# A decoder layer with 64 experts: the token table made by one-hot matmuls on chip for every batch, softplus passes moved between slots, routing steps reordered

## The chip, the cores and the metric

The kernel runs on one core of a Trainium2 chip. The metric is device time in microseconds (us) of one execution; lower is better. A core has TensorE (PE, matrix products), VectorE (DVE), ScalarE (ACT), GpSimd (POOL) and SyncE (SP), which run their own instruction queues in order and meet at semaphores.

## The reference, cut to what matters

```python
x = _layernorm(x + attn(x))                       # lightning attention, 16 heads, chunks of 128
x = _layernorm(x + mamba(ctx_1024, x))            # selective scan, below
x = _layernorm(x + ffn(x))                        # 64 experts, below
...
# mamba: B=4, L=512, inner 512, state 16
dt = jax.nn.softplus(dt + dt_proj_b[None, :, None])
def step(state, inp):
    d, b, c, u = inp
    dA = jnp.exp(d[..., None] * A)
    state = state * dA + (d * u)[..., None] * b[:, None, :]
    y = jnp.einsum('bdn,bn->bd', state, c)
...
# ffn: 2048 tokens, top 8 of 64 experts, 256 places an expert
topw, topi = jax.lax.top_k(probs, K)
flat_e = topi.reshape(-1)
oh = jax.nn.one_hot(flat_e, E, dtype=jnp.int32)
pos = jnp.take_along_axis(jnp.cumsum(oh, axis=0), flat_e[:, None], axis=1)[:, 0] - 1
xe = jnp.zeros((E, C, H), x.dtype).at[flat_e, pos].set(x_rep, mode='drop')
```

Each choice of a token gets the next place at its expert; a choice behind the 256th is dropped. The kernel needs the inverse: for each of the 64 x 256 slots, the token that sits in it (or a spare row, where the slot is empty).

## The kernel before

It has two blocks. `mixers` computes attention, scan and routing for 4 batches of 512 tokens; `experts` then gathers the token rows of one expert after another, multiplies, and adds the results to the token rows by indirect DMAs.

In `mixers` the selective scan sets the frame. A batch has 4 tiles (of the 512 inner channels), a tile 8 slots, so there are 128 slots. In each slot GpSimd makes one product (`inputs`, two partition groups at once, 128x1024), ScalarE makes two exponentials (`decays`), VectorE runs two scans and one product (`scan`), and TensorE sums over the state (`sum_states`). Every other piece of work is written by hand between these, engine by engine, in the loops `for b, for c (tile), for k (slot)`. The products are at most three slots apart from the sums (`WORK`), the decays two from the scan.

Other work in the slots: the attention of 128 tokens per tile (projections, rotation on GpSimd in slot 5, scores, values, first norm); in tile 2 the convolution for the next batch; in tile 3 the softplus of half of the next batch's channels (`EARLY`), in tile 0 that of the other half (`LATE`); in tiles 0 and 1 the second norm and the routing of the batch before.

The softplus is `soften` (ScalarE), `exponentials` (ScalarE), `logs` (ScalarE: one logarithm and two Identity passes a channel tile), `soft_parts` (GpSimd), `excess` (ScalarE), `soft_rest` (GpSimd), `steps` (ScalarE), `steps_of_u` (GpSimd); then SyncE copies the result to other partitions (`copy_steps`), which the next products and decays wait for (`spread`).

PSUM for everything but the scan is a ring of three banks: `to_fill` takes the next bank and waits until its last content was drained, in the order in which TensorE fills them.

The routing (VectorE): `shift_logits`, `choose` (top 8), `count_places` on TensorE, `find_slots` (slot number of each choice), `tell_slots`. For batches 0 to 2 the tokens are then written to a table in memory by indirect DMAs from GpSimd (`scatter`), 32 a batch of 128 entries, spread over later slots:

```python
if b and c >= 2 and UNIT * c + k >= 2 * UNIT + 2:
    scatter(b - 1, sent, sent + 1)
...
if b >= 2 and c < 2:
    each = 2 if c == 1 and k >= 6 else 1
    scatter(b - 2, sent, sent + each)
```

The last batch is done on chip: `split_slots` compares the number of each choice with 16 high and 16 low values of each expert (VectorE), ScalarE multiplies the low ones by the token number, TensorE multiplies both, VectorE masks and sums, and the list goes to memory. `experts` loads the table and that list, merges them, turns them on TensorE, and has `tokens`, which the gathers read.

## Time and profile before

| | |
|---|---|
| runs | 1347.1, 1347.75, 1350.49 us (median 1347.75) |
| profiled execution | 1349.46 us, its span 1347.6 us |
| mean granted TensorE clock | 0.875 |
| busy, us of the span | PE 1138.9, DVE 1100.1, ACT 853.8, POOL 1003.9 |
| last drain of the scan (`take_y`) | starts at 757.29 us |
| first gather of the expert part | starts at 805.45 us |

A profile row of the kind "line engine op" groups instructions of one source line; a timeline row names one instruction or a few in a row, and in brackets the idle time before it and the instruction that ended it. Times are from the start of the span.

### The profile page before, as it was taken

How to read it: one execution, taken by the hardware profiler on the slowest of the kernel's cores; microseconds unless marked ns; L12 is line 12 of the kernel's file. 1: busy time of each engine (PE TensorE's matmuls, PEld its weight loads, DVE VectorE, ACT ScalarE, POOL GpSimd, SP SyncE). 2: the span in 40 equal slices, each digit the busy share in tenths (PEclk: the TensorE clock that was granted, in tenths of full speed). 3: DMA queues.
4: the chain of work that ended last, by engine and by line, in shares of the span. 5: the costliest groups of instructions: out<-in, count | busy, mean ns of one | idle time of the engine just before them, and what ended most of it. 6: DMA issues, size and time to landing. Idle time of an engine off the chain costs nothing. (4 is left out here: it accounts for less than half of the span.)

```text
span 1347.6 us, 19321 instructions
## 1 busy us (share of the span) xinstructions
PE 1138.9 (85%) x6389; PEld 757.4 (56%) x6389; DVE 1100.1 (82%) x1536; ACT 853.8 (63%) x1536; POOL 1003.9 (74%) x796
## 2 busy tenths in 40 slices
PE   7489997898979779967887718999999999999950
PEld 2234443354424434433443418999999999999940
DVE  2379988989968799878798566998888989898846
ACT  5474585734756444847345326888878888888843
POOL 0778768777899997999988744777777777777644
PEclk9698887997889789878978658999999999999985
DMA  6525425323242432163133306999999999999978
GB/s 244 140 72 191 110 65 145 99 70 83 49 111 61 124 84 51 46 154 106 38 83 102 98 13 208 302 315 305 308 304 306 305 313 301 313 301 311 285 138 326
DMA packets 97490, 235.26 MB, mean 175 GB/s; under 512 B 20704, under 2 KB 21216, under 8 KB 96752
## 3 DMA queue, kind: packets, MB, share of 16 engines
q1 hardware_dynamic: 65648, 162.66, 39.5%
q0 software_dynamic: 31744, 71.37, 22.3%
q8 instruction: 52, 0.85, 0.3%
q14 instruction: 46, 0.38, 0.1%
HBM read 147.48 MB, written 52.94 MB: 149 GB/s over the span
## 5 line engine op out<-in xcount | busy, mean ns | idle before, releaser
L1226 DVE TENSOR_TENSOR_SCAN hst<-hst,dbu 128x512 f32<-128x512 f32 x256 | 299.2, 1214 | 97.1 <-POOL dbu L1035 71.8
L1035 POOL TENSOR_TENSOR dbu<-rep,bc 128x1024 f32<-128x1024 f32 x128 | 301.8, 2360 | 64.1 <-PE y_ps L396 35.3
L1642 POOL DMA_INDIRECT sum_rows<-ye,tokens x128 | 205.5, 1606 | 98.4 <-ACT ye L1721 75.6
L396 PE MATMUL y_ps<-dbu,cs 128*32 128x512 f32 x512 | 167.8, 741 | 70.3 <-DVE dbu L1232 62.6
L799 ACT ACTIVATE hst<-rep,small_sb 128x512 f32<-128x512 f32 x256 | 165.9, 685 | 56.8 <-DVE dbu L1232 51.5
L1634 POOL DMA_INDIRECT xe<-x_rows,tokens x128 | 150.6, 1176 | 61.4 <-issue 37.8
L434 PE MATMUL ring<-first_raw,xT 128*128 128x512 f32 x384 | 176.7, 604 | 0.5 <-DVE x2T L1314 0.5
L1232 DVE TENSOR_TENSOR dbu<-hst,bc 128x1024 f32<-128x1024 f32 x128 | 156.7, 1224 | 4.4
L1684 PE MATMUL low<-xh,w1h 128*128 128x256 f32 x512 | 150.5, 294 | 0.0
L1684 PE MATMUL low<-xh,w1l 128*128 128x256 f32 x512 | 145.3, 284 | 0.0
L1684 PE MATMUL low<-xl,w1h 128*128 128x256 f32 x512 | 145.2, 284 | 0.0
L1797 DVE TENSOR_TENSOR w1l<-first_raw,w1h 128x1024 fp32r<-128x1024 f32 (+1 forms) x128 | 117.0, 955 | 9.2 <-ACT w1h L1739 0.4
L434 PEld LDWEIGHTS ring<-first_raw,xT 128*128 128x128 f32 x384 | 69.3, 190 | 96.4 <-issue 96.4
L1140 POOL DMA_INDIRECT slot_table<-tok_i,idx_s x96 | 100.0, 1041 | 18.9 <-issue 18.1
L1790 DVE TENSOR_TENSOR xl<-turn,xh 128x512 fp32r<-128x512 f32 x128 | 82.7, 686 | 34.2 <-ACT xh L1731 33.4
L1739 ACT ACTIVATE w1h<-first_raw 128x1024 fp32r<-128x1024 f32 (+1 forms) x128 | 101.0, 844 | 8.0 <-PEq L143 8.0
L1684 PEld LDWEIGHTS low<-xl,w1h 128*128 128x128 f32 x512 | 98.6, 193 | 0.0
L396 PEld LDWEIGHTS y_ps<-dbu,cs 128*32 128x32 f32 x512 | 20.7, 118 | 138.6 <-DVE dbu L1232 78.7
L1684 PEld LDWEIGHTS low<-xh,w1h 128*128 128x128 f32 x512 | 98.5, 192 | 0.1
L1684 PEld LDWEIGHTS low<-xh,w1l 128*128 128x128 f32 x512 | 98.4, 192 | 0.0
L455 PEld LDWEIGHTS ring<-qT,kT 32*128 32x128 f32 x512 | 52.3, 296 | 70.1 <-ACT qT L774 36.3
L455 PE MATMUL ring<-qT,kT 32*128 32x128 f32 x512 | 60.9, 407 | 26.2 <-ACT kT L774 26.2
(198 smaller groups left out, 2680.0 us busy)
## 6 DMA issues: line engine op xcount, KB each, us to landing
first_raw<-in_gate_up SPq DMA_DIRECT2D x64, 768.0 KB, 9.8
rep<-made SPq DMA_DIRECT2D x256, 128.0 KB
second_raw<-in_down SPq DMA_DIRECT2D x64, 256.0 KB, 5.1
bc<-bc_rows SPq DMA_DIRECT2D x64, 128.0 KB, 3.2
second_raw<-in_down SPq DMA_DIRECT2D x64, 128.0 KB, 7.2
rows<-sum_rows SPq DMA_DIRECT2D x16, 512.0 KB, 8.9
sum_rows<-x2T SPq DMA_DIRECT2D x1, 4608.0 KB, 17.2
xT<-in_x_turned SPq DMA_DIRECT2D x16, 256.0 KB, 3.0
```

What stands on the lines that cost most here:

```text
L396: ins = pe.matmul(y_ps[rows, :], sel, dbu[:, n % WORK, g, :], start=(k == 0), stop=(k == QUADS - 1))
L434: ins = pe.matmul(ps[:, :], xT[:, t % 2, k, :], wqkv[:, "qkv".index(name), k, :], start=(k == 0), stop=(k == KD - 1))
L455: ins = pe.matmul(ps[:, g * P:(g + 1) * P], kT[r * HD:(r + 1) * HD, g, :], qT[r * HD:(r + 1) * HD, g, :], start=True, stop=True)
L799: act.activation(hst[:, at % HBANKS, :], rep[:, i % 2, g, 0, :], ACT.Exp, scale=a_sc[:, 4 * m + 2 * half + g, k:k + 1]).then_inc(da_ready, 1)
L1035: pool.tensor_tensor(dbu[:, n % WORK, :, :], rep[:, i % 2, :, 1, :], bc[:, k, 0, :].unsqueeze(1).broadcast_to([P, 2, T]), ALU.mult).then_i ...
L1226: dve.tensor_tensor_scan(h, h, dbu[:, n % WORK, i, :], 0.0, ALU.mult, ALU.add).then_inc(scanned, 1)
L1232: dve.tensor_tensor(dbu[:, n % WORK, :, :], hst[:, first:first + 2, :], bc[:, k, 1, :].unsqueeze(1).broadcast_to([P, 2, T]), ALU.mult).the ...
L1634: pool.indirect_dma_start(xe[:, e % RAW, j, :], None, x2_dram, bass.IndirectOffsetOnAxis(ap=tokens[:, e, j:j + 1], axis=0))\
L1642: pool.indirect_dma_start(sum_dram[e % SUMS], bass.IndirectOffsetOnAxis(ap=tokens[:, e, j:j + 1], axis=0), ye[:, e % YE, j, :], None, comp ...
L1684: ins = pe.matmul(dst, w[:, s, k, at:at + P], x[:, s, k, :], start=(k == 0 and n == 0), stop=(k == KD - 1 and n == 2))
L1739: act.activation(w1h[:, e % 2, :, cols], w1[:, e % RAW, :, cols], ACT.Copy).then_inc(w1h_ready, 1)
L1797: dve.tensor_tensor(w1l[:, e % 2, :, cols], w1[:, e % RAW, :, cols], w1h[:, e % 2, :, cols].bitcast(F32), ALU.subtract).then_inc(w1l_ready, 1)
```

## The change

1. The table in memory, its clearing, its 96 indirect DMAs, the last batch's list and the loading and merging in `experts` are gone. `tokens` is kept on chip from the start of the kernel and is summed up in float32.
2. For each choice, the slot number is split in its upper part (which of the 128 columns) and its lower 7 bits (which partition). `number_slots` makes both. `make_hots` (GpSimd) compares them with the numbers 0 to 127: for a slice of 128 tokens 8 one-hot rows of each kind, float16. `number_lows` (ScalarE) multiplies the low ones by token number + 1. `place_tokens` (TensorE) multiplies the two kinds and sums over the 8 choices, `add_slots` (VectorE) adds the 128x128 result to `tokens_f`. Batches 0 and 1 are placed in tiles 0 to 2 of the batch two later (`AHEAD`), batch 2 in tiles 2 and 3 of batch 3 (`AT_LAST`), the last batch behind the scan, with VectorE making the one-hots (`place_last`).
3. Softplus: `logs` keeps the logarithms alone; the Identity passes are `rounded`, one slot later. `soft_parts` of the second channel tile moves behind the last products of the tile; `rotate` in tile 3 moves from slot 5 to slot 6, and in slot 6 the step product comes behind the scan's product. `gate_z` and `gate` of channel tile 2 move to the next batch's tile 0.
4. Routing: the first two row transposes stand a step earlier, the exponentials a slot earlier, `count_places` a slot later.

```diff
-ROUTE_STEPS = 25
-LAST_STEPS = 15
+ROUTE_STEPS = 27
+HOT_OPS = 2 * NT
+AHEAD = ((0, 0), (0, 1), (0, 6), (1, 0), (1, 2), (1, 3), (1, 7), (2, 0))
+AT_LAST = ((2, 2), (2, 3), (2, 4), (2, 6), (2, 7), (3, 0), (3, 2), (3, 3))
+HOTS = {SLOT_COUNT * (r + 2) + UNIT * c + k: (r, op) for r in range(B - 2) for op, (c, k) in enumerate(AHEAD)}
+HOTS.update({SLOT_COUNT * (B - 1) + UNIT * c + k: (B - 2, op) for op, (c, k) in enumerate(AT_LAST)})
+def hots_due(n, later):
+    r, op = HOTS.get(n - later, (0, 0))
+    return ((r, op // 2),) if op % 2 else ()
...
# TensorE
+            def place_tokens(r, j):
+                pe.wait_ge(lows_numbered, NT * r + j + 1)
+                ps = to_fill(pe, f"slots{r}_{j}")
+                for k in range(TOPK):
+                    ins = pe.matmul(ps[:, 0:P], hot[:, hot_place(r, j), 1, k, :], hot[:, hot_place(r, j), 0, k, :],
+                                    start=(k == 0), stop=(k == TOPK - 1))
+                ins.then_inc(fill_sem(f"slots{r}_{j}"), 1)
...
                     sum_states(n + 1)
+                    for r, j in hots_due(n + 1, 2):
+                        place_tokens(r, j)
+                    if back and c == 1:
+                        for j in range(2):
+                            turn_rows(b - 1, j)
...
                     sum_states(n + 4)
+                    project_out(t)
+                    sum_states(n + 5)
                     if back and c == 1:
                         count_places(b - 1)
-                    project_out(t)
-                    sum_states(n + 5)
...
# ScalarE
             def logs(b, tiles):
+                act.wait_ge(soft_steps, 4 * (MI * b + tiles[0]) + 2 * len(tiles))
+                for m in tiles:
+                    act.activation(ln[m], acc[:, m, :], ACT.Ln, bias=1.0)
+
+            def rounded(b, tiles):
                 done = 4 * (MI * b + tiles[0]) + 2 * len(tiles)
-                act.wait_ge(soft_steps, done)
                 for n, m in enumerate(tiles):
-                    act.activation(ln[m], acc[:, m, :], ACT.Ln, bias=1.0)
                     act.activation(dtu_of(m), acc[:, m, :], ACT.Identity, bias=ones[:, 0:1]).then_inc(soft_steps, 1)
...
+            def number_lows(r, j):
+                act.wait_ge(hots_made, HOT_OPS * r + 2 * j + 2)
+                lows = hot[:, hot_place(r, j), 1, :, :]
+                act.activation(lows, lows, ACT.Copy, scale=cs[:, C_TOK + NT * r + j:C_TOK + NT * r + j + 1])\
+                    .then_inc(lows_numbered, 1)
...
                     decays(n + 5)
                     if soft:
-                        excess(b + 1, 0)
-                    if back and c == 1:
-                        exponents(b - 1)
+                        rounded(b + 1, EARLY)
                     take_squares(t)
...
+                    if soft:
+                        excess(b + 1, 0)
...
                     decays(n + 7)
+                    if c == 0:
+                        rounded(b, LATE)
...
# GpSimd
+            def make_hots(r, op):
+                j, low = divmod(op, 2)
+                pool.wait_ge(placed, r + 1)
+                for q, i in hot_last_in(r, j):
+                    full(pool, f"slots{q}_{i}")
+                for k in range(TOPK):
+                    ins = pool.tensor_scalar(hot[:, hot_place(r, j), low, k, :], cs[:, C_COUNT:C_COUNT + P],
+                                             place_of[:, r % 2, low, j, k:k + 1], None, ALU.is_equal)
+                ins.then_inc(hots_made, 1)
...
-                        if c == NT - 1 and k == 6 and not last:
-                            steps_of_u(b + 1, 0)
                         if n + 1 < SLOT_COUNT * B:
                             inputs(n + 1)
+                        if n in HOTS:
+                            make_hots(*HOTS[n])
...
-                        if k == 4 and c == NT - 1 and not last:
+                        if k == 5 and c == NT - 1 and not last:
                             soft_parts(b + 1, 0)
-                        if k == 5 and c == NT - 1 and not last:
                             soft_rest(b + 1, 0)
-                        if k == 6 and c == NT - 1 and not last:
-                            soft_parts(b + 1, 1)
-                        if k == 7 and c == NT - 1 and not last:
-                            soft_rest(b + 1, 1)
                         if k == 5:
                             mixed_root(t)
-                        if k == 5 and t + 1 < NT * B:
+                        if k == 6 and c == NT - 1 and not last:
+                            steps_of_u(b + 1, 0)
+                        if k == 6 and t + 1 < NT * B and c == NT - 1:
+                            rotate(t + 1)
+                        if k == 5 and t + 1 < NT * B and c < NT - 1:
                             rotate(t + 1)
-                        if k in (6, 7) and c == 0:
-                            soft_parts(b, k - 4)
+                        if k == 7 and c == NT - 1 and not last:
+                            soft_parts(b + 1, 1)
+                            soft_rest(b + 1, 1)
+                        if k == 7 and c == 0:
+                            for m in LATE:
+                                soft_parts(b, m)
...
# VectorE
+            def add_slots(r, j):
+                use = f"slots{r}_{j}"
+                ps = full(dve, use)
+                if r or j:
+                    taken(dve, f"slots{r}_{j - 1}" if j else f"slots{r - 1}_{NT - 1}")
+                dve.tensor_tensor(tokens_f, ps[:, 0:P].rearrange("p (e j) -> p e j", j=CJ), tokens_f, ALU.add)\
+                    .then_inc(drain_sem(use), 1)
+
+            def place_last(own):
+                own.settle()
+                dve.wait_ge(placed, B)
+                for j in range(NT):
+                    for k in range(TOPK):
+                        high, low = (place_of[:, (B - 1) % 2, h, j, k:k + 1] for h in range(2))
+                        dve.tensor_scalar(hot_last[:, j, 0, k, :], count16, high, None, ALU.is_equal)
+                        ins = dve.tensor_scalar(hot_last[:, j, 1, k, :], count16, low,
+                                                cs[:, C_TOK + NT * (B - 1) + j:C_TOK + NT * (B - 1) + j + 1],
+                                                ALU.is_equal, ALU.mult)
+                    ins.then_inc(hots_made, 1)
...
                     scan(n)
+                    for r, j in hots_due(n, 4):
+                        add_slots(r, j)
...
-            assert chain["route"].n == LAST_STEPS, chain["route"].n
-            split_slots()
+            find_slots(B - 1, chain["route"])
+            number_slots(B - 1, chain["route"])
+            place_last(chain["route"])
```

After every `decays(n + i)` on ScalarE stands `number_lows` for what is due two slots after its one-hots, and after every `scan(n + i)` on VectorE `add_slots` for what is due four after.

## Rows read from the trace of the kernel before

**Rows 1.** Busy time in windows cut at `take_y`; us, then busy PE, PEld, DVE, ACT, POOL.
```profile
179.13:222.24 43.11, 34.77 (x162) 14.62 (x163) 32.86 (x32) 29.46 (x46) 34.41 (x23) 0.85 0.32 80
...
264.37:312.04 47.67, 41.11 (x213) 21.72 (x213) 41.58 (x69) 20.73 (x36) 36.91 (x30) 0.86 0.41 116
...
444.59:499.36 54.77, 44.01 (x229) 24.08 (x229) 44.63 (x70) 22.88 (x40) 50.61 (x43) 0.84 0.36 100
499.36:543.89 44.53, 43.74 (x170) 17.60 (x172) 42.57 (x47) 26.81 (x41) 34.42 (x28) 0.89 0.27 63
543.89:588.56 44.67, 35.24 (x162) 15.02 (x164) 32.88 (x33) 29.41 (x46) 40.98 (x31) 0.84 0.31 76
...
686.69:724.10 37.41, 33.73 (x162) 15.71 (x160) 33.95 (x36) 18.39 (x29) 32.84 (x24) 0.86 0.32 67
724.10:757.29 33.19, 23.75 (x104) 9.57 (x104) 29.27 (x31) 15.61 (x22) 27.53 (x25) 0.71 0.31 105
```

**Rows 2.** Groups by line, GpSimd, from 60 to 757 us.
```profile
L1035 POOL TENSOR_TENSOR dbu<-rep,bc 128x1024 f32<-128x1024 f32 x125 | 294.8, 2360 | 64.1 <-PE y_ps L396 35.3 <-DVE hst L1226 15.1 <-issue 6.3
L1140 POOL DMA_INDIRECT slot_table<-tok_i,idx_s x78 | 79.8, 1023 | 13.7 <-issue 12.8 <-DVE hst L1226 0.7 <-PE y_ps L396 0.2
...
L1062 POOL TENSOR_SCALAR rms<-ssq 128x1 f32<-128x1 f32 x16 | 3.2, 202 | 1.3
```

**Rows 3.** Timeline of ScalarE at the start.
```profile
56.45 2.56 ACT L785 ACTIVATE second_raw<-second_raw,small_sb 128x512 f32<-128x512 f32 x4 [3.86 <-DMA second_raw<-in_wo]
```

**Rows 4.** Timeline of batch 2, tile 3: TensorE (first row) and GpSimd.
```profile
556.39 3.70 PE L434 MATMUL ring<-first_raw,xT 128*128 128x512 f32 x8
...
560.95 1.27 POOL L1040 TENSOR_TENSOR made<-made,acc 128x512 f32<-128x512 f32 x1 [0.93 <-ACTq L840]
...
566.95 1.27 POOL L1046 TENSOR_TENSOR made<-made,ctxT 128x512 f32<-128x512 f32 x1
...
574.34 1.27 POOL L1052 TENSOR_TENSOR made<-made,u_sb 128x512 f32<-128x512 f32 x1
...
582.66 2.34 POOL L1035 TENSOR_TENSOR dbu<-rep,bc 128x1024 f32<-128x1024 f32 x1 [1.14 <-DMA rep<-made]
```

**Rows 5.** Timeline of VectorE, places where it waited.
```profile
565.76 2.35 DVE L1226 TENSOR_TENSOR_SCAN hst<-hst,dbu 128x512 f32<-128x512 f32 x2 [3.39 <-ACT hst L799]
...
585.04 2.35 DVE L1226 TENSOR_TENSOR_SCAN hst<-hst,dbu 128x512 f32<-128x512 f32 x2 [3.47 <-POOL dbu L1035]
...
624.42 2.35 DVE L1226 TENSOR_TENSOR_SCAN hst<-hst,dbu 128x512 f32<-128x512 f32 x2 [1.33 <-ACT hst L799]
...
660.96 0.42 DVE L1319 TENSOR_REDUCE small<-x2T 128x4 f32<-128x256 f32 x1 [2.50 <-ACT x2T L887]
```

**Rows 6.** Timeline, start: small operations of VectorE, one of GpSimd.
```profile
19.71 0.16 DVE L1411 CAST below<-cs 128x128 f16<-128x128 f32 x1
19.79 0.16 DVE L1412 CAST tok_i<-cs 128x16 int32<-128x16 f32 x1
...
45.01 0.72 POOL L1111 TENSOR_TENSOR qk<-rot 128x256 f32<-128x256 f32 x1
```

**Rows 7.** Timeline, from the last slots to the first gather, all engines.
```profile
762.17 0.95 POOL L1140 DMA_INDIRECT slot_table<-tok_i,idx_s  x1 [0.30 <-issue]
...
783.23 9.17 DVE L1390 TENSOR_TENSOR bc<-x2T,cs 128x1024 f16<-128x1024 int32 x8
...
786.34 1.01 PE L558 MATMUL ring<-bc 128*128 128x128 f16 x8 [4.99 <-ACT bc L1021]
...
794.92 1.01 DVE L1399 TENSOR_REDUCE slots_of<-acc 128x64 f32<-128x512 f32 x1
795.96 0.37 SPq L763 DMA_DIRECT2D last_slots<-slots_of  x1
...
801.04 1.57 ACT L1739 ACTIVATE w1h<-first_raw 128x1024 fp32r<-128x1024 f32 x2 [8.03 <-PEq L143]
...
805.45 1.74 POOL L1634 DMA_INDIRECT xe<-x_rows,tokens  x1 [15.62 <-DVE tokens L1847]
```

More of the change, by code:

```diff
@@ L802, in first_tap @@
             def first_tap(b, m):
-                if m == 0:
-                    wait(act, routed, b - 1)
+                if b >= 3:
+                    full(act, f"slots{b - 3}_{m // 2 * 2 + 1}")
                 if m == 0 and b == 0:
@@ L936, in _ @@
                         gate_z(b, 1)
-                    if c == 3:
+                    if c == 3 and last:
                         gate_z(b, 2)
+                    if back and c == 1:
+                        take_rows(b - 1, 0)
+                        take_rows(b - 1, 1)
                     decays(n + 3)
+                    for r, j in hots_due(n + 3, 2):
+                        number_lows(r, j)
                     if front:
@@ L1353, in find_slots, with number_slots @@
                 for j in range(NT):
[L1354 to L1356 removed]
+                    own.step(dve.max(idxf[:, j, :], key[:, j, :]))
+            def number_slots(b, own):
                 own.settle()
[L1358 to L1359 removed]
+                own.step(dve.tensor_scalar(slot_i[:, 0, :, :], idxf[:, :, :], float(P - 1), None, ALU.add))
+                own.settle()
+                wait(dve, hots_made, HOT_OPS * (b - 1))
+                own.step(dve.tensor_scalar(slot_i[:, 1, :, :], slot_i[:, 0, :, :], 7, None, ALU.arith_shift_right))
+                own.step(dve.tensor_scalar(slot_i[:, 2, :, :], slot_i[:, 0, :, :], P - 1, None, ALU.bitwise_and))
+                own.settle()
+                own.step(dve.tensor_scalar(place_of[:, b % 2, 0, :, :], slot_i[:, 1, :, :], -1.0, None, ALU.add))
+                dve.tensor_copy(place_of[:, b % 2, 1, :, :], slot_i[:, 2, :, :]).then_inc(placed, 1)
+                assert own.n == ROUTE_STEPS, own.n
@@ new lines, in add_slots @@
+            def add_slots(r, j):
[6 more added lines that the diff above has]
+            def place_last(own):
+                own.settle()
+                dve.wait_ge(placed, B)
+                for j in range(NT):
+                    for k in range(TOPK):
+                        high, low = (place_of[:, (B - 1) % 2, h, j, k:k + 1] for h in range(2))
[4 more added lines that the diff above has]
+                    ins.then_inc(hots_made, 1)
+                taken(dve, f"slots{B - 2}_{NT - 1}")
+                ps = full(dve, f"slots{B - 1}")
+                spares = key[:, 0:2, :].rearrange("p j e -> p (j e)").rearrange("p (e j) -> p e j", j=CJ)
+                own.step(dve.tensor_tensor(tokens_f, ps[:, 0:P].rearrange("p (e j) -> p e j", j=CJ), tokens_f, ALU.add))
+                own.settle()
+                own.step(dve.scalar_tensor_tensor(out=spares, in0=tokens_f, scalar=0.0,
+                                                  in1=cs[:, C_SPARE:C_SPARE + CJ].unsqueeze(1).broadcast_to([P, EXPERTS, CJ]),
@@ L1360, in tell_slots @@
                                                   op0=ALU.is_equal, op1=ALU.mult))
                 own.settle()
-                wait(dve, scattered, 16 * NT * TOPK * b)
-                own.step(dve.tensor_scalar(spill_f[:, :], spill_f[:, :], float(T * TOPK), None, ALU.add))
-                dve.scalar_tensor_tensor(out=idx_s[:, :].rearrange("p (j k) -> p j k", j=NT), in0=idxf[:, 0, :, :],
-                                         scalar=-1.0, in1=idxf[:, 1, :, :], op0=ALU.add, op1=ALU.add).then_inc(routed, 1)
@@ L1402, in _ @@
+                dve.scalar_tensor_tensor(out=tokens[:, :, :], in0=tokens_f, scalar=-1.0, in1=spares,
+                                         op0=ALU.add, op1=ALU.add).then_inc(tokens_ready, 1)
             dve.memset(ones[:, :], 1.0)
```

264 lines of the change are left out of this document (94 added, 170 removed).

## Prediction, made before the changed kernel had run

> **What bounds the kernel now.** I read first the chain of waits on the page: its end is the expert part, mostly TensorE products of one expert after another. The diff leaves that part as it is except for its first lines, so I take it as a block that starts earlier or later; the first gather starts at 805.45 [rows 7] and the span is 1347.6, so the block is 542 us. All the rest is the time until that gather. The profiled execution's own time is 1349.46, 1.7 above the median of the three timed runs (1347.75); I work with differences and set them on the profiled 1349.46.
>
> Second I read busy time in windows that are cut at the end of each 8-slot tile of the selective scan (the y drain of VectorE) [rows 1]. The reader should see three kinds of tile. Where batch b+1 is convolved (batch 2, tile 2) TensorE is busy 43.7 of 44.5 us and GpSimd only 34.4: GpSimd's work is covered there. Where the softplus of the next batch runs (tile 3) VectorE is busy 32.9 of 43 to 45 us, so a chain of waits sets the time. Where the routing of the batch before runs (tile 1) the time is 47.7 in batch 1, which sends no scatters, and 54.8 in batches 2 and 3, with 10 scatters in the tile: GpSimd is then busy 50.6. Batch 3's tiles 2 and 3 have neither convolution nor softplus and are near VectorE's own work, 37.4 and 33.2.
>
> Third, groups by line on GpSimd [rows 2]: a product for the scan costs 2.36 us and each slot needs one; a scatter is 1.02 busy and 0.18 idle behind it, so 1.2 a piece. 78 lie within the scan, the rest behind it.
>
> **Change 1: scatters out, one-hots in (GpSimd).** Removed are 78 x 1.2 = 94 us of GpSimd time. Added are 24 calls of make_hots, each 8 compares of 128x128 with one float32 input and a float16 output: 192 instructions. No row has this form. Below, a 128x1 tensor_scalar takes 0.20 [rows 2]; above, a two-input add of 128x256 takes 0.72, issued every 0.68 [rows 6], that is 0.20 and 2.0 ns an element, so a two-input 128x128 would take 0.45. With one operand instead of two I halve the slope: 0.20 + 0.13 - 0.04 of overlap = 0.29, rounded to 0.30, 2.4 us a call, 58 us in all. The ends are 1.6 and 3.6 us a call.
> The totals favour the change by 36 us, but scatters came one a slot, while the calls come as lumps. They lie: batch 2 tiles 0 and 1, 3 and 4 calls; batch 3 the same; tile 2 of batch 2, 1; tiles 2 and 3 of batch 3, 6 and 3. Batch 1's tiles 2 and 3, and batch 2's tile 3, only lose scatters.
> On this price the Trainium skill speaks (GPSIMD Engine Reference, Engine selection): a one-input operation on GpSimd runs about at line rate, a two-input one at about half of VectorE's speed. Its 1.2 GHz would make the element part 0.11 and not 0.13, an estimate of 0.27 a piece and some 5 us less in the sum below; the slope of the two-input row speaks for the same direction.
>
> Laid out slot by slot (VectorE 3.55 for the two scans and the product, plus its extras; GpSimd 2.36 plus its extras, at most two slots ahead):
> - Tiles 0 and 1 of batches 2 and 3. Three calls (7.2) replace eight scatters (9.6), then four (9.6) ten (12.0). The relief is small, and two of the calls stand in slots 0 and 1, where the decayed keys, the step product and the gate are due too. With change 2 and 3 in it I get -2.8 for each pair, -5.5.
> - Batch 2 tile 2: TensorE bound; the placing of one slice adds 8 matmuls. Those of this shape took 1.01 for eight [rows 7]. Its PSUM bank is kept until VectorE adds it two slots later, and the third fill behind it waits: +1.5.
> - Batch 3 tile 2: GpSimd's 32.8 busy less 6.1 of scatters plus 14.4 of calls is 41, against 37.4 for the tile; its lead and the time of the call made early cover part: +1.6. Tile 3: 27.5 less 8.2 plus 7.2 seems covered, but the tile starts with no lead, and the call of slot 0 and 2 pushes the products: +3.2.
> - 12 scalings on ScalarE of 128x1024 (two passes of that size take 1.57 [rows 7], so 0.8 each) and 12 adds on VectorE (0.3 each): ScalarE is busy 23 of 55 us in such tiles and hides them; the adds are in the sums above.
> At 0.45 a compare instead of 0.30, nine calls in batch 3's end and seven in each pair cost 1.2 us more, and about 25 us of it shows; at 0.20 some 13 come back.
>
> **Change 2: the softplus in other slots.** Rows 5 show what it aims at: in batch 2 tile 3 the fifth slot's scan waited 3.39 for ScalarE, which ran the logs and four Identity passes before the decays. Now the passes run after the decays. But rows 4 show the chain that ends last in this tile: half 0's parts at 560.95, its rest at 566.95, the step product at 574.34, the copy of the steps to the other partitions, landed at 582.66, and the product for the next batch's first scan. That chain: after the change q's copy ends at 560.7 (its products end at 560.1 [rows 4]), the table load of 1.28 and the decays of 1.25 follow, so the Identity passes start at 563.2 and the parts, two passes later, at 564.65 (+3.7); parts, rest and root run to 569.9, the slot's product to 572.2, the step product ends 573.45 instead of 575.6; the copy takes 7.05, landed 580.5 (-2.15). Then comes what is new. The product (2.35) goes first, and only behind it the parts of half 1 (2.45); ScalarE's excess of half 1 (0.63) waits for these, and the decays of the next batch's first slot are queued behind the excess on ScalarE. The scan starts at 580.5 + 2.35 + 2.45 + 0.63 + 0.75 = 586.7 against 585.04 [rows 5]: +1.65. So the stall that is removed is paid back 20 us later. Batches 1 and 2: +1.65 each; batch 0, which had no scatters (tile 43.1 against 44.7), comes to the same length: +3.2. Sum +6.5.
> In tile 0 the wait for ScalarE before the eighth scan (1.33 in batch 3 [rows 5]) goes: -1.5 in batch 1, and an estimated -2.5 in batch 0, where ScalarE has the load of the start beside it; batches 2 and 3 are in the pairs above.
> At the start, GpSimd's step product of half 0 comes 1.1 earlier, and so does everything SyncE queues behind its copy, the load of the output weights among it (ScalarE waits 3.86 for it [rows 3]); the first product comes some 2 us later, since half 1's whole chain now runs behind the rotation and ahead of it, but the second scan waits for ScalarE behind the weights anyway: -1.
>
> **Change 3: the routing.** The rows turn earlier and the exponentials stand before q's copy; the 2.50 that VectorE waits for them in tile 1 [rows 5] goes: -2.4 in batch 1, in the pairs for the others.
>
> **Change 4: the tail.** Before, VectorE spends 783.23 to 795.93 on comparing and packing slots, then the list goes out to memory and back, and the gather starts at 805.45 [rows 7]. The next block opened at 801.04, 2.9 after the store landed (795.96 and 2.1). After: find_slots and number_slots from 781.4 end about 785.9 (256-wide operations at 0.42, 32-wide at 0.18). Then 64 compares of 128x128 in float16. Below: casts of that size are issued every 0.08 [rows 6]; above: each lasts 0.16. I take 0.09, for nothing waits between them: 5.8, so 791.7; last matmuls 1.3, three 128x128 operations 1.1: 794.1; the blocks' change 2.9: 797.0. Gain 8.45. Besides, three scatters stood before the first row's root on GpSimd (the last from 762.17 to 763.12 [rows 7], while the statistics were ready at 762.3): 0.85. Sum -9.3.
> For these compares the Trainium skill has a rule that speaks against them (VectorE: DVE Perf Modes, The TRN2 errata): a fixed cost for every instruction with an SBUF source, 58 cycles by its table but about 150 measured, so small tiles are to be avoided. By the first, 64 cost 6.0; by the second (an estimate) 12.2. The casts side with the first.
>
> **Sum**: start -1; batch 0 -2.5 + 3.2; batch 1 -1.5 - 2.4 + 1.65; batch 2 -2.8 + 1.5 + 1.65; batch 3 -2.8 + 1.6 + 3.2; tail -9.3. That is -9.5, so 1349.5 - 9.5 = 1340; on the median 1338. I give 1339.
>
> **Rivals.**
> A. Compares are cheap (0.20 to 0.25): GpSimd stops binding in tiles 0 and 1 of batches 2 and 3, whose tile 1 falls towards batch 1's 47.7. For: 128x1 costs 0.20. Gives -15 to -23, 1326 to 1334.
> B. Compares near 0.36: mixers +8, tail -9: no change, 1345 to 1352.
> C. Slower: compares at 0.45 a piece, the two-input slope, which GpSimd's compare with a pointer scalar and a conversion may well have. It decides from 0.38 on, in batch 3 tiles 2 and 3. The sum is -9.5 + 25 = +15, 1365; halfway 1356.
> D. The tail's compares run at their full 0.16 with no overlap: 10.6 instead of 5.8, gain 4.7 less: 1344. The page's 150 cycles (the Trainium skill, same section) would be 6.4 less.
> E. The late exponentials and passes are not what binds: then tiles 3 do not change at all and the sum is 6 lower, 1333.
>
> **Numbers.** My forecast with E (1333 to 1343) 0.42; A 0.18; B and D 0.21; C 0.19. A difference within 0.3% (4 us) is about what a measurement of this kernel can't tell from none. Faster: forecast all but 0.02, A, and a part of D, 0.62; same 0.19; slower C, 0.19. The range leaves out the far ends of A and C: 1324 to 1354.
>
> **What would show it.** Compares at 0.25 to 0.35 and no scatter in GpSimd's groups; tile 3 of batches 0 to 2 all near 46, with the last scan's wait for ScalarE; tile 1 of batch 1 near 45; the last 16 slots of batch 3 some 5 longer, waiting for GpSimd; the first gather 39 us after the last y drain and not 48. Wrong it gets by the compares' price first, and by the PSUM bank that each placed slice holds for two slots, which I priced at 1.5 only where TensorE binds.

## The result and the profile after

The kernel after takes 1409.29 us (median of four, 1407.4 to 1413.0) against 1349.11: a ratio of 1.0451, 95% interval 1.0423 to 1.0479. It is 60 us slower, and I had forecast 10 us faster, with 1354 as the upper end. Times here and below are medians over the fast runs; one run of wide_sub at 1414 us, one at 5956 and one of best at 3723 were slow and are left out. The profiled execution took 1410.18 (span 1408.2). Its expert part, first gather to end, is 542.4 us as before; the loss lies ahead of the first gather, which starts at 865.84 instead of 805.45.

Busy time in windows cut at the y drain, kernel after (columns as in [rows 1]); by row: batch 0 tile 3, batch 1 tile 1, batch 2 tiles 0 to 3, batch 3 tiles 2 and 3:

```profile
180.54:226.29 45.75, 31.75 (x166) 13.90 (x168) 32.76 (x32) 26.89 (x43) 33.66 (x24) 0.93 0.37 94
267.58:314.07 46.49, 40.26 (x223) 21.64 (x219) 43.00 (x72) 21.59 (x37) 38.17 (x30) 0.89 0.40 114
403.71:457.80 54.09, 41.57 (x180) 19.25 (x179) 39.11 (x47) 30.28 (x46) 47.03 (x53) 0.78 0.25 64
457.80:519.88 62.08, 46.74 (x243) 25.15 (x240) 52.30 (x73) 23.77 (x39) 57.72 (x65) 0.82 0.31 87
519.88:565.29 45.41, 43.24 (x178) 17.87 (x180) 42.77 (x48) 27.93 (x42) 31.09 (x26) 0.92 0.23 53
565.29:611.91 46.62, 34.89 (x166) 15.46 (x168) 32.86 (x33) 26.79 (x43) 33.81 (x23) 0.86 0.37 92
727.73:778.35 50.62, 38.86 (x176) 18.59 (x176) 34.55 (x38) 21.55 (x32) 50.10 (x61) 0.78 0.27 72
778.35:822.86 44.51, 25.58 (x128) 10.96 (x128) 30.08 (x34) 17.67 (x24) 36.36 (x43) 0.65 0.15 47
```

Beside [rows 1] the reader should see two kinds of tile. Those without calls of make_hots moved by 3 us at most. Those with calls grew by 7 to 13, and in them GpSimd (last busy column) is at 47 to 58 us: in batch 3's tile 2 at 50.10 of 50.62, where it was 32.84 of 37.41. In batch 3's last tile it is at 36.36 of 44.51 only, but there it works without a gap over 0.1 us from 779.38 to 814.15. Batch 2's tile 2, with one call, grew by 0.9 only. What VectorE waited for in batch 3's tile 2 (us in total, times, longest), kernel before, then after:

```profile
DVE hst L1226 <- POOL dbu L1035: 1.8, 1, 1.8
```

```profile
DVE hst L1268 <- POOL dbu L1083: 15.7, 5, 4.4
```

GpSimd's groups by line, kernel after:

```profile
L1083 POOL TENSOR_TENSOR dbu<-rep,bc 128x1024 f32<-128x1024 f32 x128 | 301.1, 2356 | 96.2 <-PE y_ps L403 49.6 <-DVE hst L1268 28.0 <-DMA rep<-made 9.4
...
L1190 POOL TENSOR_SCALAR acc<-cs,place_of 128x128 f16<-128x128 f32 x192 | 112.5, 608 | 0.0
```

The product costs what it did [rows 2]. The 192 compares are busy 608 ns each, issued every 0.58 (eight in 4.66 us), where I had taken 0.30. That is 112 us in place of the scatters' 94.

Length of the tiles in all kernels whose traces are read below (us between y drains, from each kernel's own timeline; "tail" is last drain to first gather):

```
               batch 0     batch 1                batch 2                batch 3
kernel         tile 3   t0    t1    t2    t3    t0    t1    t2    t3    t0    t1    t2    t3   tail
before          43.1   42.1  47.7  44.3  44.6  43.6  54.8  44.5  44.7  43.3  54.8  37.4  33.2  48.2
after           45.8   41.3  46.5  43.9  45.8  54.1  62.1  45.4  46.6  54.1  61.7  50.6  44.5  43.0
dve_hots        45.7   41.5  46.6  43.9  51.2  61.3  53.0  45.4  52.2  61.1  53.0  52.9  36.5  43.0
bank_later      45.7   41.5  46.6  43.9  45.8  51.1  59.8  53.0  46.6  51.1  59.8  55.5  43.6  43.0
split_calls     45.8   41.5  46.6  43.9  45.8  54.2  58.9  50.7  46.6  52.5  58.4  50.7  45.7  42.3
decays_first    45.9   40.4  47.5  43.9  45.8  50.4  65.5  45.4  46.4  50.4  65.8  50.7  44.6  43.0
wide_sub        45.7   41.4  46.5  43.9  45.7  44.1  53.4  47.5  47.6  44.1  52.3  39.1  37.5  43.0
act_hots        46.8   41.1  46.4  43.9  45.9  48.5  53.6  45.4  46.4  48.8  52.0  39.8  37.4  43.0
orders          45.8   41.4  46.2  43.9  47.4  44.8  52.9  43.9  47.2  44.8  55.2  37.7  33.3  47.9
routing         42.0   42.4  45.4  43.8  43.2  44.0  54.3  43.9  43.1  44.0  54.3  37.4  33.1  48.4
parts_first     42.0   41.9  46.3  43.9  43.8  45.4  53.0  43.9  44.6  45.4  53.0  37.8  31.5  47.6
best            41.8   42.0  46.5  43.9  41.9  44.6  53.4  47.5  43.9  44.6  52.1  39.1  37.5  40.4
best2           41.9   41.9  46.5  43.9  41.9  44.6  55.5  45.5  41.9  44.6  55.6  37.4  34.5  40.4
```

Timeline of VectorE in the tail, kernel after, and the first gather:

```profile
850.17 0.25 DVE L1424 TENSOR_SCALAR bc<-xT,place_of 128x128 f16<-128x128 f16 x1
850.34 0.31 DVE L1425 TENSOR_SCALAR bc<-xT,place_of,cs 128x128 f16<-128x128 f16 x1
850.57 0.25 DVE L1424 TENSOR_SCALAR bc<-xT,place_of 128x128 f16<-128x128 f16 x1
...
862.30 0.30 DVE L1425 TENSOR_SCALAR bc<-xT,place_of,cs 128x128 f16<-128x128 f16 x1
863.80 0.29 DVE L1432 TENSOR_TENSOR tokens<-ring,tokens 128x128 f32<-128x128 f32 x1 [1.20 <-PE ring L568]
...
865.84 1.24 POOL L1674 DMA_INDIRECT xe<-x_rows,tokens  x1 [32.09 <-POOLq L159]
```

The starts give the price: 0.17 behind a compare, 0.23 behind the compare that also multiplies, 12.4 us for the 64. The tail gained 5.2 us, not 9.3.

### The profile page after: what moved, and what is told of

Its sections match the earlier page's. It is cut to its first block and busy times, and to the rows that moved or that the text cites. A ratio compares the mean times of both kernels' runs of the same rounds, so it can differ in the third digit from the quotient of the medians.

```text
span 1408.2 us, 19706 instructions
## 1 busy us (share of the span) xinstructions
PE 1147.8 (82%) x6484; PEld 764.8 (54%) x6484; DVE 1119.8 (80%) x1614; ACT 853.3 (61%) x1526; POOL 1014.3 (72%) x892
## 5 line engine op out<-in xcount | busy, mean ns | idle before, releaser
L403 PE MATMUL y_ps<-dbu,cs 128*32 128x512 f32 x512 | 159.7, 707 | 66.8 <-DVE dbu L1274 51.7
L441 PE MATMUL ring<-first_raw,xT 128*128 128x512 f32 x384 | 188.6, 637 | 5.3 <-DVE tokens L1415 3.4
L441 PEld LDWEIGHTS ring<-first_raw,xT 128*128 128x128 f32 x384 | 73.9, 203 | 103.0 <-issue 103.0
L1190 POOL TENSOR_SCALAR acc<-cs,place_of 128x128 f16<-128x128 f32 x192 | 112.5, 608 | 0.0
L462 PE MATMUL ring<-qT,kT 32*128 32x128 f32 x512 | 57.3, 388 | 56.8 <-ACT kT L798 56.8
L462 PEld LDWEIGHTS ring<-qT,kT 32*128 32x128 f32 x512 | 49.2, 280 | 92.6 <-ACT qT L798 67.6
```

Of the source, the lines that this page charges most:

```text
L403: ins = pe.matmul(y_ps[rows, :], sel, dbu[:, n % WORK, g, :], start=(k == 0), stop=(k == QUADS - 1))
L441: ins = pe.matmul(ps[:, :], xT[:, t % 2, k, :], wqkv[:, "qkv".index(name), k, :], start=(k == 0), stop=(k == KD - 1))
L1190: ins = pool.tensor_scalar(hot[:, hot_place(r, j), low, k, :], cs[:, C_COUNT:C_COUNT + P], place_of[:, r % 2, low, j, k:k + 1], None, ALU. ...
```

## The experiments

**The price by itself (probe).** Added ahead of the first softplus; the groups left out are the same with a float32 output, an immediate scalar, a float16 input, a multiplication, and four of 256 elements:

```diff
+            for k in range(8):
+                pool.tensor_scalar(at16[:, k * P:(k + 1) * P], count, ptr[:, k:k + 1], None, ALU.is_equal)
...
+            for k in range(2):
+                pool.tensor_tensor(in16[..., 8 * P], count.unsqueeze(1).broadcast_to([P, 8, P]),
+                                   ptr.unsqueeze(2).broadcast_to([P, 8, P]), ALU.subtract)
```

> The kernel after with operations added ahead of its first softplus on GpSimd, eight of a form (four or two of the wide ones), and behind its first convolution on VectorE, so that the disputed price is measured by itself; the added results are not used. Theory P1 (every GpSimd instruction has a large fixed part, the width counts little): 128x128 compares cost 0.5 to 0.6 us in every form and the 256 wide one under 0.8. Theory P2 (the pointer scalar costs): with an immediate scalar they fall to about 0.3. Theory P3 (the rounding to float16 costs): with a float32 output they fall to about 0.3. Theory P4 (the comparison itself costs): the multiplication with the same operands takes about 0.3. One broadcast subtraction of 8x128 takes 2.1 to 2.4 us. On VectorE I expect 0.19 a piece for the one-operation compare from float16 and 0.17 to 0.25 from float32, 1.15 for the one broadcast compare of 8x128, and the two-input additions beside GpSimd's compares held up by microseconds instead of taking 0.35.

Groups by line, GpSimd alone (busy, mean ns), then VectorE alone, except for L1225 and L1509, which ran side by side:

```profile
L1225 POOL TENSOR_SCALAR dbu<-cs 128x128 f16<-128x128 f32 x8 | 5.5, 705 | 7.8 <-DVE y L1504 7.8
L1206 POOL TENSOR_SCALAR kv<-cs 128x128 f32<-128x128 f32 x8 | 4.7, 603 | 0.0
L1214 POOL TENSOR_SCALAR dbu<-cs 128x128 f16<-128x128 f32 x8 | 4.7, 609 | 0.0
L1203 POOL TENSOR_SCALAR dbu<-cs 128x128 f16<-128x128 f32 x8 | 4.7, 600 | 12.9 <-DMA cs<-in_table 12.9
L1211 POOL TENSOR_SCALAR dbu<-dbu,cs 128x128 f16<-128x128 f16 x8 | 4.6, 592 | 0.0
L1208 POOL TENSOR_SCALAR dbu<-cs 128x128 f16<-128x128 f32 x8 | 4.0, 517 | 0.0
L1219 POOL TENSOR_TENSOR x<-cs 128x1024 f16<-128x1024 f32 x2 | 3.8, 1894 | 0.0
L1216 POOL TENSOR_SCALAR dbu<-cs 128x256 f16<-128x256 f32 x4 | 3.6, 925 | 0.0
...
L1500 DVE TENSOR_TENSOR y<-cs 128x1024 f16<-128x1024 f32 x2 | 2.4, 1220 | 0.0
...
L1509 DVE TENSOR_SCALAR x<-cs 128x128 f16<-128x128 f32 x8 | 1.7, 299 | 0.0
L1493 DVE TENSOR_SCALAR pr<-cs 128x128 f16<-128x128 f32 x8 | 1.7, 279 | 23.9 <-POOL x L1219 23.9
...
L1495 DVE TENSOR_SCALAR pr<-below,cs 128x128 f16<-128x128 f16 x8 | 1.4, 248 | 0.0
```

The busy time over the count is the price. The comparison (L1203) costs what the multiplication (L1214) costs, with either output (L1206) and either input (L1211): P3 and P4 fall. An immediate scalar (L1208) saves 0.09 of 0.58: P2 holds for a seventh. P1 half holds: every form of 128 costs 0.50 to 0.58, but 256 elements take 0.91 against 0.58, where it wanted less than 0.8; so 0.25 is fixed and an element costs 2.6 ns, while the two-input subtraction costs 1.8 ns an element. A one-input operation is thus not cheaper per element than a two-input one. Here the Trainium skill (GPSIMD Engine Reference, Engine selection: one-input roughly at line rate) does not agree with the measurement. One broadcast subtraction of 1024, which takes 1.87, leaves only the turning of differences into one-hots to do, and that can go elsewhere. VectorE's prices came as expected (0.21 from float32, 0.17 from float16, 1.18 for the broadcast compare). The expected hold-up did not: the pair of additions of 256 elements (L1507) took 0.76 us, as long as the pair ahead of it, though its last 0.57 us ran beside GpSimd's compares.

**The new order alone (orders).** Kernel before with changes 2 and 3 of the prediction (the softplus passes, the routing).

> The kernel before with changes 2 and 3 alone (the softplus passes spread over slots, the routing reordered); scatters and the old tail are kept. Theory T1 (the price of GpSimd's compares is the loss): batches 0 and 1 of the kernel after, which have no compares, are 3 us longer in sum than before, so this kernel comes out at +0 to +4 us, 1349 to 1353. Rival R3 (the new order is the loss, because GpSimd's softplus work now stands in the same slots as other work in batches 2 and 3): +15 or more, 1365 or above.

1351.96 us, ratio 1.0031 (1.0012 to 1.0050). R3 falls: the order costs 4 us of the 60, none of it in batch 3's last tiles.

**The compares on VectorE (dve_hots).** make_hots moved, word for word, behind the scan of the same slot:

```diff
                     scan(n + 1)
                     for r, j in hots_due(n + 1, 4):
                         add_slots(r, j)
+                    if n + 1 in HOTS:
+                        make_hots(*HOTS[n + 1])
```

> The kernel after with the same 192 compares issued by VectorE, behind the scan of the same slot, instead of GpSimd; placing, scaling and adding stay. Theory T1: GpSimd no longer binds, tiles 0 and 1 of batches 2 and 3 fall from 54 and 62 us to 44 to 47 and 48 to 51; the last two tiles of batch 3, near VectorE's own work, pay the compares there (9 calls at 1.6 us) and come to 42 to 46 and 37 to 40 instead of 50.6 and 44.5. In all 1348 to 1360. Rival R2 (the PSUM bank that a placed slice holds for two slots stalls TensorE and through it the rotation): that stays as it is, tiles 0 and 1 stay above 52 and 58, and the time stays above 1390.

1408.94 us, ratio 1.0451 (1.0423 to 1.0480): no faster than after. By the number that I had written down this spoke for R2. The tiles say otherwise: tiles 1 fell from 62 to 53, near what T1 wants, and the loss moved to tiles 0 (61) and to tile 3 of batches 1 and 2 (51 and 52), whose y drain now stands behind the first call of the next tile. Timeline of dve_hots, first GpSimd, then VectorE:

```profile
441.09 4.71 POOL L1083 TENSOR_TENSOR dbu<-rep,bc 128x1024 f32<-128x1024 f32 x2
445.84 1.27 POOL L1088 TENSOR_TENSOR made<-made,acc 128x512 f32<-128x512 f32 x1
447.07 1.26 POOL L1089 TENSOR_TENSOR ctxT<-made,ctxT 128x512 f32<-128x512 f32 x1
448.30 1.26 POOL L1088 TENSOR_TENSOR made<-made,acc 128x512 f32<-128x512 f32 x1
449.52 1.26 POOL L1089 TENSOR_TENSOR ctxT<-made,ctxT 128x512 f32<-128x512 f32 x1
...
443.43 8.02 DVE L1404 TENSOR_SCALAR acc<-cs,place_of 128x128 f16<-128x128 f32 x8
451.38 0.74 DVE L1315 SCALAR_TENSOR_TENSOR x<-ring,rms,x_in 128x512 f32<-128x512 f32 x1
```

The trace shows no wait for another engine here. The eight compares, 1.7 us in the probe, last 8.02, and they end just after GpSimd's unbroken row of two-input operations does (450.78). Taken one by one (shortest, median and longest in ns):

```profile
L1404 DVE TENSOR_SCALAR acc<-cs,place_of x8: 274/1302/2454, 443.4 to 451.2; 128x128 f16<-128x128 f32 x8
```

The first five took 2.45, 1.38, 1.30, 1.31 and 1.30 us, each until one more of GpSimd's five instructions had ended; the last three, behind the row, took 0.28. Over all 24 calls VectorE was busy for 88 us where the work is 40. So the experiment did not test what it was made for: it put in the place of GpSimd's price a stall of VectorE behind GpSimd. The Trainium skill (SBUF — State Buffer, Who interferes with whom) says that such pairs exclude each other for the length of an instruction; for these compares the trace agrees, one of them for each GpSimd instruction. Beside GpSimd's compares there was no such stall (L1509 in the probe, 1.75 us for eight against 1.66), but GpSimd's slowed from 0.58 to 0.69.

**The bank held for one slot (bank_later).** The placing matmuls one slot later:

```diff
-                    for r, j in hots_due(n, 2):
+                    for r, j in hots_due(n, 3):
                         place_tokens(r, j)
```

> The kernel after with the eight placing matmuls of a slice one slot later on TensorE, so that the PSUM bank is held for one slot instead of two; GpSimd's compares are the same. Theory T1: within 3 us of the kernel after, 1406 to 1413. Rival R2 (the bank held): at least a third of the loss goes, 1390 or less.

1408.01 us, ratio 1.0465 (1.0425 to 1.0506): no change in the sum, as T1 says, but not for the reason that nothing happened. Tiles 0 and 1 of batch 2 became 3.0 and 2.3 shorter, and tile 2 of batches 2 and 3 became 7.6 and 4.9 longer. GpSimd's waits in batch 2 tile 0, kernel after, then bank_later:

```profile
POOL rot L1155 <- issue: 5.3, 1, 5.3
```

```profile
POOL rot L1155 <- ACT qk L798: 3.1, 1, 3.1
```

In the kernel after TensorE placed a slice at 427.65, had to wait for a bank until VectorE's sum ended at 430.9, and so projected k late; the rotation waited 5.3 us, and it started when k's copy was done. TensorE's rows for that projection, kernel after, then bank_later:

```profile
431.06 5.37 PE L441 MATMUL ring<-first_raw,xT 128*128 128x512 f32 x8 [0.29 <-DVE x L1338]
```

```profile
423.09 3.67 PE L441 MATMUL ring<-first_raw,xT 128*128 128x512 f32 x8 [1.04 <-DVE x L1338]
```

So the bank is not all of it: the projection itself took 1.7 us more, at a granted clock of 0.68 (in part at the lower of TensorE's two levels) against 1.00, as it did in batch 3's tile 0 too (5.37 against 3.67). Bank and clock together cost each pair of tiles some 5 us; how they share it was not tested. Where the later placing falls into the convolution it costs more than it saves.

**Less time on GpSimd (wide_sub), and none (act_hots).**

```diff
-                for k in range(TOPK):
-                    ins = pool.tensor_scalar(hot[:, hot_place(r, j), low, k, :], cs[:, C_COUNT:C_COUNT + P],
-                                             place_of[:, r % 2, low, j, k:k + 1], None, ALU.is_equal)
+                ins = pool.tensor_tensor(hot[:, hot_place(r, j), low, :, :],
+                                         cs[:, C_COUNT:C_COUNT + P].unsqueeze(1).broadcast_to([P, TOPK, P]),
+                                         place_of[:, r % 2, low, j, :].unsqueeze(2).broadcast_to([P, TOPK, P]), ALU.subtract)
...
+                act.activation(both, both, ACT.Square)
+                act.activation(both[:, 0], both[:, 0], ACT.Relu, bias=ones[:, 0:1], scale=-1.0)
+                act.activation(both[:, 1], both[:, 1], ACT.Relu, bias=tok, scale=neg)
```

> The kernel after with the eight compares of a call on GpSimd replaced by one broadcast subtraction of 8x128 elements (number minus place), which the probe showed at 1.87 us against 4.66; ScalarE turns the differences into one-hots with a squaring of 2048 elements and two Relu passes of 1024 a slice, about 3.9 us where one pass of 1.15 stood. GpSimd gets 24 x 2.8 = 67 us back, and no run of its instructions is longer. Theory T1 (GpSimd's occupation by the calls is most of the loss of 60): most of the +10.5, +7, +13 and +11 in the tiles of batches 2 and 3 goes, and the time is 1355 to 1375. Rival R2 (what each slice costs on TensorE and in held PSUM banks) and rival R5 (the calls are in the wrong slots, whatever they cost): above 1390.

1354.01 us, ratio 1.0040 (1.0010 to 1.0069), the fast end of T1's range. Busy time in windows of wide_sub, batch 2 tiles 0 to 2 and batch 3 tiles 2 and 3:

```profile
402.72:446.83 44.11, 38.22 (x180) 18.03 (x179) 39.12 (x48) 33.44 (x48) 38.73 (x32) 0.85 0.30 77
446.83:500.24 53.41, 43.81 (x243) 24.04 (x240) 49.02 (x74) 29.74 (x43) 47.01 (x35) 0.85 0.35 101
500.24:547.78 47.54, 44.05 (x178) 17.93 (x180) 42.86 (x49) 31.09 (x44) 27.59 (x21) 0.90 0.22 51
691.80:730.88 39.08, 34.38 (x160) 15.38 (x160) 34.38 (x38) 27.62 (x34) 34.89 (x23) 0.84 0.27 63
730.88:768.37 37.49, 25.27 (x144) 12.20 (x144) 29.90 (x34) 26.68 (x33) 25.32 (x20) 0.73 0.26 86
```

With the slots, the placing and the banks unchanged, some 3 us more a slice on ScalarE and 67 us less on GpSimd, 55 us come back (53 by the tiles of batches 2 and 3); batch 3's tile 2 falls from 50.6 to 39.1 as GpSimd's busy time falls from 50.1 to 34.9. This is the test that dve_hots failed to be, and R2 and R5 fall as main causes. In tiles 0 no projection is slow any more (3.67 to 3.70 us); what the clock has in the 55 is not known apart.

In act_hots GpSimd makes nothing; ScalarE makes each call, ahead of a Relu pass:

```diff
+                for k in range(TOPK):
+                    ins = act.activation(hot[:, hot_place(r, j), low, k, :], cs[:, C_COUNT:C_COUNT + P], ACT.Square,
+                                         bias=place_of[:, r % 2, low, j, k:k + 1])
```

> The kernel after with the one-hots made on ScalarE alone: eight squarings of 128x128 with the place as a bias, then one Relu pass of 1024, about 3.5 us a call; GpSimd makes none, and VectorE none. Theory T1: with no call on GpSimd, tiles 0 and 1 of batches 2 and 3 come to batch 1's length, 44 and 47, plus what ScalarE's decays are late; batch 3's last tiles come to 38 to 42 and 33 to 37. 1345 to 1365. Rival R2 (TensorE and PSUM): above 1390. Rival R6 (ScalarE becomes the bound, its 3.5 us lumps ahead of the decays stop the scan): 1370 to 1400, with VectorE waiting for ScalarE.

1359.83 us, ratio 1.0090 (1.0068 to 1.0112): T1's range again. Something of R6 is in it: tile 0 of batch 2 is at 48.5 against wide_sub's 44.1, and VectorE waits 4.2 us there for the decays. With the calls cheaper on GpSimd, or off it and off VectorE too, most of the loss is gone: it was GpSimd's occupation.

**Lumps or total (split_calls).** Four compares in one slot, four in the next:

```diff
+                        if n - 1 in HOTS:
+                            make_hots(*HOTS[n - 1], range(TOPK // 2, TOPK))
                         if n in HOTS:
-                            make_hots(*HOTS[n])
+                            make_hots(*HOTS[n], range(TOPK // 2))
```

> The kernel after with each call of eight compares on GpSimd cut in two: four compares (2.33 us) behind one slot's product, four behind the next slot's. The 192 compares and their price are the same. Theory T7 (the lumps: 4.66 us in one slot is more than GpSimd's lead over the scan, the total of 112 us is not the matter): 1375 to 1395. Rival T8 (the total occupation of GpSimd in tiles 0 and 1 of batches 2 and 3 is what counts, it is the bound there slot for slot): 1400 to 1412, as the kernel after.

1405.83 us, ratio 1.0421 (1.0401 to 1.0442). T7 falls and T8 holds: a pair of tiles became 3 to 5 us shorter, the tile behind it in batch 2 5.3 longer, and the sum is near after's. What counts is mainly the total.

**ScalarE's queue (decays_first).** On the kernel after:

```diff
-                    if c == 0:
-                        excess(b, 2)
                     if more:
                         decays(n + 8)
                         for r, j in hots_due(n + 8, 2):
                             number_lows(r, j)
+                    if c == 0:
+                        excess(b, 2)
```

> The kernel after with one edit on ScalarE: in the last slot of tile 0 the decays of the next slot are issued ahead of the softplus excess that waits for GpSimd's parts, and no longer behind it. In the kernel after, VectorE waited 5.7 us there for the decays in batch 2. If that wait sets the time, tile 0 of batches 2 and 3 comes 3 to 6 us shorter each, and the whole 1398 to 1403; if GpSimd's own occupation is the bound and ScalarE only shows it, tiles 0 and 1 together keep their 116 us and the time stays at 1406 to 1412.

1408.28 us, ratio 1.0442 (1.0420 to 1.0465). Tile 0 of batch 2 became 3.7 us shorter and tile 1 3.4 longer: 115.9 for both against 116.2. The 5.7 us wait of VectorE for ScalarE is gone and was worth nothing: in the same tile VectorE now waits 9.0 us for GpSimd's products, where it waited 6.9.

**The softplus parts ahead of the product (parts_first), and the routing alone (routing).** On orders, and on before:

```diff
+                        if k == 6 and c == NT - 1 and not last:
+                            soft_parts(b + 1, 1)
...
                         if k == 7 and c == NT - 1 and not last:
-                            soft_parts(b + 1, 1)
                             soft_rest(b + 1, 1)
```

> The kernel with changes 2 and 3 alone (orders), with one edit: GpSimd makes the softplus parts of half 1 at the end of the seventh slot of tile 3, behind the rotation, and no longer behind the next batch's first product. My account of tile 3 (the product goes first, the parts follow, ScalarE's excess waits for them and the first decays are queued behind it) says that the 2.5 to 2.8 us that tile 3 of batches 0 to 2 lost in orders go: 44.5 or less, 1343 to 1348. If instead the later step product or the rotation moved to the seventh slot is what costs, tile 3 stays at 46 to 47.

1341.84 us, ratio 0.9948 (0.9927 to 0.9969); tile 3 falls from 45.8, 47.4, 47.2 to 42.0, 43.8, 44.6. Timeline of orders at the end of batch 2's tile 3:

```profile
580.97 2.33 POOL L1047 TENSOR_TENSOR dbu<-rep,bc 128x1024 f32<-128x1024 f32 x1 [2.11 <-DMA rep<-made]
...
583.27 1.25 POOL L1052 TENSOR_TENSOR made<-made,acc 128x512 f32<-128x512 f32 x1
584.49 1.25 POOL L1053 TENSOR_TENSOR ctxT<-made,ctxT 128x512 f32<-128x512 f32 x1
...
585.77 0.63 ACT L850 ACTIVATE ctxT<-ctxT 128x512 f32<-128x512 f32 x1 [11.69 <-POOL ctxT L1053]
586.31 1.29 ACT L802 ACTIVATE hst<-rep,small_sb 128x512 f32<-128x512 f32 x2
...
587.09 1.23 DVE L1240 TENSOR_TENSOR_SCAN hst<-hst,dbu 128x512 f32<-128x512 f32 x1 [10.87 <-ACT hst L802]
```

This is the order that the prediction wrote down: product, parts, excess, decays, scan. With the parts ahead, the decays were done and the scan waited for the product alone.

> The kernel before with change 3 alone (the routing reordered: rows turned earlier, exponentials ahead of q's copy, place counts later, the third gate moved to the next tile 0). I expect tile 1 of batch 1 at 46.3 instead of 47.7, tile 1 of batch 2 at 53 instead of 54.8, nothing in tile 3, and 1342 to 1346 in all, which makes change 2 as written a loss of 5 to 9 us in the kernel orders. Rival: the routing is worth nothing and the whole of the softplus change is too: 1347 to 1351.

1341.77 us, ratio 0.9963 (0.9941 to 0.9985). Change 3 alone is a gain of some 5 us (2 to 8 by the interval). Its tile 1 of batch 1 is 2.3 shorter where I had expected 1.4, and tile 1 of batch 2 0.5 shorter where I had expected 1.8; tile 3 of batches 0 to 2 is 1.1 to 1.6 shorter, which I had not expected: the third gate left it. Change 2 as written costs about 4 us in each of these tiles (orders against routing). Even with the parts ahead it gains nothing: parts_first has both changes and is no faster than routing, which has change 3 alone.

**Putting it together (best, best2).** In the tail of best:

```diff
-                        dve.tensor_scalar(hot_last[:, j, 0, k, :], count16, high, None, ALU.is_equal)
+                        if j < 2:
+                            dve.tensor_scalar(hot_last[:, j, 0, k, :], count16, high, None, ALU.is_equal)
```

with the high one-hots of slices 2 and 3 on ScalarE; best2 finishes each half of the one-hots separately.

> The kernel after with three edits: the broadcast subtraction of wide_sub, the softplus parts of half 1 ahead of the next batch's product (parts_first), and in the tail the high one-hots of the last two slices made on ScalarE (eight squarings and one Relu pass a slice), so that VectorE has 48 compares and not 64. By the sum of the tiles: wide_sub's 1355 less 3.7, 2.0 and 3.0 in tile 3 of batches 0 to 2, less 16 x 0.17 = 2.7 in the tail: 1344 (1340 to 1348), against 1349 of before and 1342 of parts_first. It beats both only if tile 3 gives back more than that.

> The kernel best with ScalarE's finishing passes spread: two slots behind each subtraction the squaring (1024 elements) and the Relu pass of that half of the one-hots, about 2.3 us a time, instead of all three passes (4.3 us) behind the second. If the lump on ScalarE is what costs batch 2's tile 2 (47.5 against 43.9 where nothing is placed) and the last two tiles of batch 3 (39.1 and 37.5 against 37.4 and 33.1), 4 to 7 us go: 1336 to 1340. If it is the placing on TensorE and the bank held, these tiles stay within 0.5 us and the time at 1341 to 1345.

1342.59 us, ratio 0.9946 (0.9925 to 0.9967), as expected, and 1341.75, ratio 0.9945 (0.9922 to 0.9967). Both beat the kernel before by half a per cent, but neither can be told from parts_first or routing. The tail is 7.8 us shorter than before's; what is left of the calls in batches 2 and 3 takes most of that back. In best2 the tiles 2 and 3 became shorter by what was expected (47.5 to 45.5, 39.1 to 37.4, 37.5 to 34.5), but tiles 1 became 2.1 and 3.5 longer, and the 1336 to 1340 that I had expected for the whole was missed.

## Why the prediction was wrong

**The price of a compare on GpSimd: the step that failed.** "With one operand instead of two I halve the slope" gave 0.30, and for its ends 0.20 and 0.45. Measured: 0.58, with a slope above the two-input row's, not half of it. Rival C had the mechanism, but stopped at the two-input slope and saw it decide in batch 3's last two tiles; these grew by 24.5 us, the two pairs of tiles 0 and 1 by 35.5. Put through the prediction's own sums, 2.26 us more a call makes 15.8 in each pair of tiles, 13.6 and 6.8 in batch 3's last two: 52 of the 60 us by which the tiles with calls missed. wide_sub, which takes most of the price away and little else, gives back 53 in these and the tiles beside them.

**The pairs of tiles 0 and 1: the PSUM bank, in part.** Forecast -2.8, measured +17.8 and +17.7; the price leaves some 5 of this open. The text named the bank and priced it only in batch 2's tile 2. There the number agrees (+0.9 for +1.5), and in the pairs the bank was forgotten: bank_later gives 5.3 and 4.9 back. A part of that, 1.7 us in the place read above, is the slower projection and not the wait. Both were read from one place of the trace and this one run, not tried with more banks. In tiles 1 there is a third thing, VectorE's stall behind GpSimd (last section), 7.57 us where the kernel before has 2.32; its share is open too.

**Batch 3, tiles 2 and 3.** Forecast +1.6 and +3.2, measured +13.2 and +11.3; with the measured price the same working gives 15.2 and 10.0.

**The softplus.** The account of tile 3 was right in its order, as parts_first shows. That the size came out too, +3.2, +1.65, +1.65 forecast, +2.7, +1.2, +1.9 measured, is luck in part: the chain costs 4 and not 1.65 to 3.2, and the gate that left, which I had not priced, gave 1.1 to 1.6 back. Tile 0 of batch 1: -0.8 for -1.5.

**The routing.** -2.4 forecast for tile 1 of batch 1; -2.3 with the routing alone, -1.2 in the kernel after. What takes back the other half is not known.

**The tail.** Forecast -9.3, measured -5.2. The term mis-sized is the VectorE compare: 0.09 taken from casts, 0.19 measured, 6.6 us; the part ahead of the compares cost 0.5 and the part behind them 2 less than taken. Of the two figures of the Trainium skill (VectorE: DVE Perf Modes, The TRN2 errata) the measured 150 cycles, an estimate of 12.2 us, was right (12.4), and I had sided with the table. This was rival D, larger than written.

**The start.** The first y drain lies between 93.6 and 100.1 in these executions, whatever the kernel; the -1 can't be judged, nor the -2.5 for batch 0's tile 0, which ends there.

The forecast's sign was wrong with 0.19 on slower. Even rival C's far end, 1365, stopped 44 us short, because its price, 0.45, was taken as a bound though no row showed this form of instruction; and the range cut that end off as well, at 1354.

## What to carry to other kernels

Where the trace does not show an instruction's form on an engine, the nearest row is no bound: leave the upper end open (here the price was twice what I took), or measure the form by itself first; the first row of the probe would have decided this case. Count what an engine has to do in a tile, not how it is lumped: once GpSimd was the bound, neither splitting the calls nor removing a 5.7 us wait on ScalarE moved the sum of the tiles. And work moved off one of VectorE and GpSimd on to the other can be paid twice; ScalarE, 18 to 30 us busy in tiles of 44 to 62, had the room.

## What the runs showed of the hardware

While GpSimd ran two-input operations one behind another, VectorE's operations with all operands in SBUF were held up, in two ways, each read at the places named and not tried by itself. The compares of dve_hots, with one tensor input, got through one for each GpSimd instruction: 8.02 us for 1.7 us of work. A two-input operation of the routing, in the kernel after, was held for a whole row of four: it took 7.57 us, 0.42 where GpSimd was idle, though it had started before the row, which ran from 487.40 to 494.50. In batch 3 it took 7.55; in the kernel before, with one such GpSimd instruction beside it, 2.32. VectorE's timeline:

```profile
487.21 7.57 DVE L1365 TENSOR_TENSOR x2T<-x2T,small 128x256 f32<-128x256 f32 x1
```

Not every operation is held. A reduction and a reciprocal just ahead of it (0.41 and 0.18) ran beside GpSimd's compares unhindered; in dve_hots the normalization statistics of 128x512 took 0.69 at 438.00, beside GpSimd's two-input rotation (437.16 to 439.66); and so with every scan, whose state lies in PSUM: its mean is 1.21 us in dve_hots and in the kernel after alike.
